# Sums of decayed traces in a two-layer conditioning and mixture kernel: additions on GpSimd against accumulating transfers within the chip

## The chip, the cores and the metric

One core of a Trainium2 chip runs the kernel. The metric is the device time of one execution in microseconds, the median of several runs. Lower is better.

## The reference, cut to what matters

The kernel computes a language-adapted feed-forward mixture over 8 batches of 512 tokens and 256 channels, then a temporal conditioning with a second mixture of 64 experts. The change touches the conditioning alone, and there this part:

```python
def causal_ema(b, tau_raw):
    alpha = jnp.exp(-jax.nn.softplus(tau_raw)).astype(b.dtype)
    def step(h, bt):
        h = alpha * h + bt
        return (h, h)
...
gated = x * wg
mod = 0.5 + jax.nn.sigmoid(jnp.einsum('bth,dh->btd', h1, Wn2) + bn2)
traces = jax.vmap(lambda tau, m: causal_ema(gated * m[..., None], tau))(tau_raws, jnp.moveaxis(mod, -1, 0))
blend_w = jax.nn.softmax(blend, axis=0)
temporal = jnp.einsum('dbtc,dc->btc', traces, blend_w)
gate = jax.nn.sigmoid(jnp.einsum('btc,ec->bte', temporal, Wtemp) + btemp)
soma = jax.nn.gelu(jnp.einsum('btc,ec->bte', x, Wsoma) + bsoma, approximate=False)
out = jnp.einsum('btc,ec->bte', soma * gate, Wout)
```

Eight time constants (D = 8) give eight traces for each batch; `temporal` is their weighted sum. The sum of traces, seven additions for each batch, is what the change moves.

## The kernel before, in words

The kernel has three stages: layer 0 (to about 538 us of the span), the conditioning of layer 1 (to about 830 us), and the 64 experts of layer 1. Five engines run programs of their own, and semaphores order them.

In the conditioning a batch is a tile of 128 partitions (channels) x 2 halves x 512 tokens in float32, 4 KB for each partition, 512 KB in all. The blend weight is folded into the input, so the traces have only to be added. For each batch `b` and each time constant `d` from 0 to 7 the work runs through three engines:

- ScalarE, `weighted` (L879), scales the gated input with the blend weight into `gb`, of which there are two buffers.
- GpSimd, `drive_of` (L628), multiplies it with the modulation `md` into one of three `drive` buffers. It waits for the scan of three drives earlier.
- VectorE, `scan_unit` (L1239), scans each half along time, two instructions for each drive. Trace 0 goes straight to `acc[b % 2]`; traces 1 to 7 go to one of three `trace` buffers, which must have been added before they are written again.
- `add_trace` adds trace `d` to `acc[b % 2]`. GpSimd does it for `d` = 1, 2, 3, 5, 6 and 7 (L636), VectorE for `d` = 4 (L1248); in the last batch VectorE also does 6 and 7. Each addition waits for its scan and for the addition before it, through the semaphore `c_add`.

When addition 7 is through, TensorE's `temp_in` projects `acc` with `wtemp` (L1629), ScalarE applies the tanh (`gate_out`, L920), and VectorE's `gate_soma` (L1270) multiplies it with `soma`. The statistics of the normalisation follow (`stats`, L1277 and L1280), then four small GpSimd instructions in `rstd_of` (L614 to L619).

The order on each engine is written out by hand, as a list in its `step(b)`, and three batches overlap in a step. GpSimd's step `b` is: `rstd_of(b - 2)`, drive 7 and addition 5 of batch `b - 1`, drives 0 and 1 of batch `b`, additions 6 and 7 of `b - 1`, drive 2, addition 1, drives 3 and 4, additions 2 and 3, drives 5 and 6 of `b`. VectorE's step has scans 0 and 1, `shared_b`, the context scan, `pick` (its cast is L1303), scan 2, `gate_soma`, scan 3, `shared_a`, `route_weights` (L1331), scan 4, `stats`, addition 4, scan 5, `gate_in` (L1263), scan 6, `finish` (L1338) and scan 7.

The sync engine's queue issues the loads and stores: the modulation, broadcast to all partitions (L435, 1 MB, twice a step), the batch's rows (L420, L446), and the stores (L451, L455). In its step 3 it also issues the first five experts' weights (L427, L428). GpSimd issues indirect transfers in the other stages (L587, L602, L713, L720) and one direct transfer with addition, of 4 MB, at the very end (L737).

Of the kernel before, what the change touches and what calls it, by code (L numbers as in the profile page):

```python
# [31 lines left out]
D = 8  # L32
# [14 lines left out]
def level(m, per=1):  # L47
    return (m + 1 + CREDIT) * per
# [15 lines left out]
def build(nc, t):  # L64
# [20 lines left out]
    with ctx:  # L85
# [241 lines left out]
        c_mst = sem("c_mst", 16)  # L327
        c_mdl = [sem(f"c_mdl{n}", 16) for n in range(2)]
        c_pad, e_pad = sem("c_pad", 0), sem("e_pad", 0)
        c_in = [sem(f"c_in{p}", 16) for p in range(2)]  # L330
# [38 lines left out]

        def added(b, d):  # L370

            return level((D - 1) * b + d - 1)

# [8 lines left out]
        def _(sp):  # L382
# [74 lines left out]
            def c_step(b):  # L457
# [18 lines left out]
                if b == B:  # L476
                    z_store(B - 2)

                    sp.wait_ge(c_add, added(B - 1, D - 1))
                    for e in range(OWN + HEADS, FREED):  # L480
                        e_load(e)
# [24 lines left out]
        def _(pool):  # L506
# [124 lines left out]
            def add_trace(b, d):  # L631
                pool.wait_ge(c_scan, level(D * b + d))
                if d > 1:
                    pool.wait_ge(c_add, added(b, d - 1))
                pool.drain()
                G.tensor_tensor(acc[b % 2][:, :, :], acc[b % 2][:, :, :], trace[((D - 1) * b + d - 1) % TRACES], ALU.add).then_inc(c_add, 1)  # L636
# [14 lines left out]
            def step(b):  # L651
# [6 lines left out]
                if ahead(b):  # L658
                    drive_of(b, 0)
                if ahead(b):  # L660
                    drive_of(b, 1)
                if on(b - 1) and b != B:
                    add_trace(b - 1, 6)
                if on(b - 1) and b != B:
# [9 lines left out]
                if on(b):  # L674
                    add_trace(b, 2)
                if on(b):
                    add_trace(b, 3)
                if on(b):
                    drive_of(b, 5)
                if on(b):  # L680
                    drive_of(b, 6)
                if b == B:

                    pool.wait_ge(c_add, added(B - 1, D - 1))
                    for r in range(FREED):
# [364 lines left out]
        def _(dve):  # L1050
# [177 lines left out]
            def scan_unit(b, d):  # L1228
# [5 lines left out]
                else:  # L1234
                    n = (D - 1) * b + d - 1
                    dve.wait_ge(c_add, level(n - TRACES))
                    dst = trace[n % TRACES]
# [5 lines left out]
            def add_trace(b, d):  # L1243
                dve.wait_ge(c_scan, level(D * b + d))
                if d > 1:
                    dve.wait_ge(c_add, added(b, d - 1))
                dve.drain()
# [253 lines left out]
        def _(pe):  # L1501
# [152 lines left out]
            def temp_in(q):  # L1654
                pe.wait_ge(c_add, added(q, D - 1))
                if q + 2 < B:
# [278 lines left out]
```

## Time and profile before

| | |
|---|---|
| median of 3 runs | 1130.76 us (1129.94 to 1133.33) |
| the profiled execution, its time | 1128.04 us |
| the profiled execution, its span | 1126.3 us |
| VectorE busy over the span | 743.0 us (66%) |
| GpSimd busy over the span | 663.5 us (59%) |
| TensorE busy over the span | 939.8 us (83%) |

The table's shares are averages over three stages with different limits. For this change only the conditioning counts, so it is to be read by its steps. In the rows, PE is TensorE, PEld its weight loads, DVE VectorE, ACT ScalarE, POOL GpSimd and SP the sync engine; "wide" is the buffer in which `drive`, `trace`, `acc`, `gb` and others lie. What stands in brackets behind a row of the timeline is the idle time ahead of it and what ended it.

### The profile page before, as it was taken

The numbers are of one execution on the slowest core, as the hardware profiler recorded it, in microseconds if no ns is written. First come the engines' busy times: TensorE is split into PE (matmuls) and PEld (weight loads), VectorE is DVE, ScalarE is ACT, GpSimd is POOL, SyncE is SP. The second block draws the span as 40 slices with busy tenths as digits, with TensorE's granted clock in tenths as the row PEclk, the third lists the DMA queues.
The fourth block names the chain that finished last, engine by engine and source line by source line (L and its number), as shares of the span: only waits on it lengthen the run. The fifth ranks groups of instructions, "written<-read, shape, count | busy, mean of one in ns | idle before, by whom it ended". The sixth has DMA issues, their size and how long they took to land. (4 is left out here: it accounts for less than half of the span.)

```text
span 1126.3 us, 15057 instructions
## 1 busy us (share of the span) xinstructions
PE 939.8 (83%) x4616; PEld 676.5 (60%) x4616; DVE 743.0 (66%) x1523; ACT 470.3 (42%) x843; POOL 663.5 (59%) x495
## 2 busy tenths in 40 slices
PE   5981399999999999988478899998777798999960
PEld 3761289998999899973134555554454465556540
DVE  3547366766676667534578999999874786777620
ACT  2331055445544555354346665666422132233320
POOL 1113415545554555325899999999850577777870
PEclk9885599999999999998689999999876999999995
DMA  2559514444443443223212652344348599997558
GB/s 78 149 185 368 157 47 90 94 117 86 89 96 77 120 90 52 29 57 108 86 51 75 214 159 87 111 136 119 104 140 317 172 254 254 270 260 152 94 72 157
DMA packets 90455, 151.28 MB, mean 134 GB/s; under 512 B 15816, under 2 KB 72848, under 8 KB 87248
## 3 DMA queue, kind: packets, MB, share of 16 engines
q1 hardware_dynamic: 55184, 95.46, 25.9%
q0 software_dynamic: 25104, 39.86, 20.5%
q10 hardware_dynamic: 10096, 15.10, 4.1%
q8 instruction: 33, 0.54, 0.2%
q14 instruction: 38, 0.31, 0.1%
HBM read 115.37 MB, written 43.42 MB: 141 GB/s over the span
## 5 line engine op out<-in xcount | busy, mean ns | idle before, releaser
L628 POOL TENSOR_TENSOR wide<-wide 128x1024 f32<-128x1024 f32 x64 | 156.5, 2459 | 32.1 <-issue 32.1
L1239 DVE TENSOR_TENSOR_SCAN wide<-bank,wide 128x512 f32<-128x512 f32 x128 | 149.4, 1209 | 21.8 <-POOL wide L628 21.8
L855 ACT ACTIVATE h_raw<-bank,b 128x512 f32<-128x512 f32 x128 | 87.9, 688 | 168.3 <-PE bank L1602 165.9
L1194 DVE TENSOR_TENSOR h_lo<-h_raw,h_hi 128x512 fp32r<-128x512 f32 x128 | 87.2, 692 | 93.9 <-ACT h_hi L859 93.9
L1617 PE MATMUL bank<-w_hi,h_hi 128*128 128x256 f32 x512 | 144.3, 282 | 0.1
L1617 PE MATMUL bank<-w_lo,h_hi 128*128 128x256 f32 x512 | 142.1, 277 | 0.0
L1617 PE MATMUL bank<-w_hi,h_lo 128*128 128x256 f32 x512 | 142.0, 277 | 0.0
L602 POOL DMA_INDIRECT x_rows<-ob,put x64 | 110.9, 1733 | 27.3 <-issue 14.3
L636 POOL TENSOR_TENSOR wide<-wide 128x1024 f32<-128x1024 f32 x46 | 108.5, 2358 | 11.9 <-issue 8.2
L879 ACT ACTIVATE wide<-wide,blend 128x512 f32<-128x512 f32 x128 | 84.1, 716 | 59.9 <-POOL wide L628 56.5
L1602 PE MATMUL bank<-ex_hi,w_hi 128*128 128x512 f32 x256 | 100.3, 392 | 4.9 <-issue 4.9
L1602 PE MATMUL bank<-ex_hi,w_lo 128*128 128x512 f32 x256 | 101.3, 396 | 0.0
L1602 PE MATMUL bank<-ex_lo,w_hi 128*128 128x512 f32 x256 | 101.0, 394 | 0.0
L1617 PEld LDWEIGHTS bank<-w_hi,h_hi 128*128 128x128 f32 x512 | 96.8, 189 | 1.6 <-issue 1.1
L1617 PEld LDWEIGHTS bank<-w_lo,h_hi 128*128 128x128 f32 x512 | 96.9, 189 | 0.3 <-issue 0.2
L1617 PEld LDWEIGHTS bank<-w_hi,h_lo 128*128 128x128 f32 x512 | 96.7, 189 | 0.0
L713 POOL DMA_INDIRECT xg<-z_rows,slots x64 | 63.5, 992 | 54.1 <-DVE slots L1377 36.1
L596 POOL COPY put<-idxT 128x4 int32<-128x4 int32 (+1 forms) x16 | 3.0, 185 | 137.8 <-DVE ob L1183 137.8
L587 POOL DMA_INDIRECT xg<-n_rows,take x64 | 67.4, 1052 | 28.2 <-issue 14.9
L859 ACT ACTIVATE h_hi<-h_raw 128x512 fp32r<-128x512 f32 x128 | 77.9, 621 | 0.0
L1038 ACT ACTIVATE ys<-bank 128x256 f32<-128x256 f32 x64 | 24.5, 383 | 98.0 <-DMA out<-ys,slots 43.3
L720 POOL DMA_INDIRECT odd_rows<-ys,slots x32 | 51.4, 1606 | 17.3 <-ACT ys L1038 8.2
(230 smaller groups left out, 2034.1 us busy)
## 6 DMA issues: line engine op xcount, KB each, us to landing
wide<-in_mwp SPq DMA_DIRECT2D x40, 512.0 KB, 4.4
wide<-m_rows SPq DMA_DIRECT2D x16, 1024.0 KB, 4.8
w1s<-in_fW SPq DMA_DIRECT2D x8, 1024.0 KB, 5.0
w2s<-in_fW SPq DMA_DIRECT2D x8, 1024.0 KB, 5.3
own<-in_mwp SPq DMA_DIRECT2D x15, 512.0 KB, 4.2
z_rows<-zrow SPq DMA_DIRECT2D x8, 640.0 KB, 7.1
head<-in_mwp SPq DMA_DIRECT2D x9, 512.0 KB, 4.4
xt<-in_x SPq DMA_DIRECT2D x8, 512.0 KB, 3.9
```

What stands on the lines that cost most here:

```text
L587: G.indirect_dma_start(xg0[p][:, j, :], None, n0_rows[:, :], bass.IndirectOffsetOnAxis(ap=take[p][:, j:j + 1], axis=0)).then_inc(b_got[p], 16)
L602: G.indirect_dma_start(x1_rows[:, :], bass.IndirectOffsetOnAxis(ap=put[p][:, j:j + 1], axis=0), ob[p][:, j, :], None, compute_op=ALU.add). ...
L628: G.tensor_tensor(drive[n % DRIVES], gb[d % 2], md[d // HD][:, d % HD, :].unsqueeze(1).to_broadcast([P, CT, S]), ALU.mult).then_inc(c_u, 1)
L636: G.tensor_tensor(acc[b % 2][:, :, :], acc[b % 2][:, :, :], trace[((D - 1) * b + d - 1) % TRACES], ALU.add).then_inc(c_add, 1)
L713: G.indirect_dma_start(xg1[i][:, :], None, z_rows[:, :], bass.IndirectOffsetOnAxis(ap=slots[:, e:e + 1], axis=0)).then_inc(e_got[i], 16)
L855: A.activation(h1_raw[f % 4][:, :], bank[:, 2 + f % 4, :], ACT.Gelu_apprx_tanh, bias=b1_0[:, bass.ds(e, 1), f]).then_inc(b_h, 1)
L859: A.activation(h1_hi[:, f - 1, :], h1_raw[(f - 1) % 4][:, :], ACT.Copy).then_inc(b_hi, 1)
L879: o = A.activation(gb[d % 2][:, c, :], gated2[b % 2][:, c, :], ACT.Copy, scale=blend[:, c, d:d + 1])
L1194: V.tensor_tensor(h1_lo[:, f, :], h1_raw[f % 4][:, :], h1_hi[:, f, :].bitcast(F32), ALU.subtract).then_inc(b_lo, 1)
L1239: o = V.tensor_tensor_scan(dst[:, c, :], decay[:, d:d + 1].to_broadcast([P, S]), drive[(D * b + d) % DRIVES][:, c, :], 0.0, ALU.mult, ALU.add)
L1602: o = T.matmul(bank[:, 2 + f % 4, :], w[q][:, at], x[p][:, c, :], start=(c == 0 and n == 0), stop=(c == CT - 1 and n == 2))
L1617: o = T.matmul(rows4(6)[:, j, :], x[:, f, rows], w[q][:, f * H:(f + 1) * H], start=(f == 0 and n == 0), stop=(f == FT0 - 1 and n == 2))
```

## The change

For all batches but the last, additions 1, 2, 3, 5, 6 and 7 are made by a transfer that GpSimd issues: it reads the trace in the chip's memory and adds it to `acc`. Each transfer adds 16 to the semaphore `c_acc` of its buffer when it has landed, and whoever waited for `c_add` waits for that. Addition 4 stays on VectorE, and the last batch is added as before. On GpSimd, addition 6 moves ahead of drive 1, and drive 5 moves ahead of addition 3.

```diff
@@ -326,6 +326,7 @@
         c_no = sem("c_no", TT)
         c_mst = sem("c_mst", 16)
         c_mdl = [sem(f"c_mdl{n}", 16) for n in range(2)]
+        c_acc = [sem(f"c_acc{p}", 0) for p in range(2)]
         c_pad, e_pad = sem("c_pad", 0), sem("e_pad", 0)
         c_in = [sem(f"c_in{p}", 16) for p in range(2)]
         c_xr, c_zst, c_ost = sem("c_xr", 16), sem("c_zst", 16), sem("c_ost", 16)
@@ -367,9 +368,17 @@
 
             return 0 < n < B
 
-        def added(b, d):
-
-            return level((D - 1) * b + d - 1)
+        BY_DMA = (1, 2, 3, 5, 6, 7)
+
+        def wait_added(eng, b, d):
+
+
+            if b == B - 1:
+                eng.wait_ge(c_add, level(B - 1 + d - 1))
+            elif b >= 0 and d in BY_DMA:
+                eng.wait_ge(c_acc[b % 2], 16 * (len(BY_DMA) * (b // 2) + BY_DMA.index(d) + 1))
+            elif b >= 0:
+                eng.wait_ge(c_add, level(b))
 
         def conditioning(first, step):
 
@@ -476,7 +485,7 @@
                 if b == B:
                     z_store(B - 2)
 
-                    sp.wait_ge(c_add, added(B - 1, D - 1))
+                    wait_added(sp, B - 1, D - 1)
                     for e in range(OWN + HEADS, FREED):
                         e_load(e)
                 if ahead(b + 1):
@@ -631,7 +640,11 @@
             def add_trace(b, d):
                 pool.wait_ge(c_scan, level(D * b + d))
                 if d > 1:
-                    pool.wait_ge(c_add, added(b, d - 1))
+                    wait_added(pool, b, d - 1)
+                if b < B - 1:
+                    pool.dma_start(acc[b % 2].rearrange("p c s -> p (c s)"), trace[((D - 1) * b + d - 1) % TRACES].rearrange("p c s -> p (c s)"),
+                                   accum_op=ALU.add).then_inc(c_acc[b % 2], 16)
+                    return
                 pool.drain()
                 G.tensor_tensor(acc[b % 2][:, :, :], acc[b % 2][:, :, :], trace[((D - 1) * b + d - 1) % TRACES], ALU.add).then_inc(c_add, 1)
 
@@ -657,10 +670,10 @@
                     add_trace(b - 1, 5)
                 if ahead(b):
                     drive_of(b, 0)
+                if on(b - 1) and b != B:
+                    add_trace(b - 1, 6)
                 if ahead(b):
                     drive_of(b, 1)
-                if on(b - 1) and b != B:
-                    add_trace(b - 1, 6)
                 if on(b - 1) and b != B:
                     add_trace(b - 1, 7)
                 if ahead(b):
@@ -674,14 +687,14 @@
                 if on(b):
                     add_trace(b, 2)
                 if on(b):
+                    drive_of(b, 5)
+                if on(b):
                     add_trace(b, 3)
-                if on(b):
-                    drive_of(b, 5)
                 if on(b):
                     drive_of(b, 6)
                 if b == B:
 
-                    pool.wait_ge(c_add, added(B - 1, D - 1))
+                    wait_added(pool, B - 1, D - 1)
                     for r in range(FREED):
                         G.memset(wdb[r][0:P - FR, :], 0.0)
                     pool.wait_ge(c_om, level(B - 1))
@@ -1233,7 +1246,7 @@
                     dst = acc[b % 2]
                 else:
                     n = (D - 1) * b + d - 1
-                    dve.wait_ge(c_add, level(n - TRACES))
+                    wait_added(dve, (n - TRACES) // (D - 1), (n - TRACES) % (D - 1) + 1)
                     dst = trace[n % TRACES]
                 for c in range(CT):
                     o = V.tensor_tensor_scan(dst[:, c, :], decay[:, d:d + 1].to_broadcast([P, S]),
@@ -1243,7 +1256,7 @@
             def add_trace(b, d):
                 dve.wait_ge(c_scan, level(D * b + d))
                 if d > 1:
-                    dve.wait_ge(c_add, added(b, d - 1))
+                    wait_added(dve, b, d - 1)
                 dve.drain()
                 V.tensor_tensor(acc[b % 2][:, :, :], acc[b % 2][:, :, :], trace[((D - 1) * b + d - 1) % TRACES], ALU.add).then_inc(c_add, 1)
 
@@ -1652,7 +1665,7 @@
                 o.then_inc(c_h1m, 1)
 
             def temp_in(q):
-                pe.wait_ge(c_add, added(q, D - 1))
+                wait_added(pe, q, D - 1)
                 if q + 2 < B:
                     pe.wait_ge(c_x1T, level(q + 2))
                 pe.wait_ge(c_fin, level(q - 2))
```

## Rows read from the trace of the kernel before

**Rows 1.** Busy time by batch step: stretch, length, engines (instructions), TensorE clock, DMA share, GB/s.

```profile
...
593.91:631.02 37.11, 34.43 (x114) 19.42 (x114) 32.84 (x51) 22.55 (x36) 35.73 (x19) 0.95 0.31 104
631.02:668.14 37.12, 33.25 (x116) 18.30 (x114) 36.09 (x54) 23.84 (x37) 35.74 (x19) 1.00 0.64 197
668.14:705.60 37.46, 34.91 (x116) 19.15 (x114) 35.85 (x54) 23.84 (x37) 35.79 (x19) 0.95 0.36 117
```

**Rows 2.** The page's costliest groups, GpSimd's drives (L628) and additions (L636).

```profile
...
L628 POOL TENSOR_TENSOR wide<-wide 128x1024 f32<-128x1024 f32 x64 | 156.5, 2459 | 32.1 <-issue 32.1
...
L636 POOL TENSOR_TENSOR wide<-wide 128x1024 f32<-128x1024 f32 x46 | 108.5, 2358 | 11.9 <-issue 8.2
```

**Rows 3.** GpSimd's timeline in one step: start, length, instruction, idle before it.

```profile
...
670.65 2.37 POOL L636 TENSOR_TENSOR wide<-wide 128x1024 f32<-128x1024 f32 x1 [0.16 <-issue]
672.98 4.65 POOL L628 TENSOR_TENSOR wide<-wide 128x1024 f32<-128x1024 f32 x2
677.79 2.36 POOL L636 TENSOR_TENSOR wide<-wide 128x1024 f32<-128x1024 f32 x1 [0.16 <-issue]
680.66 2.35 POOL L636 TENSOR_TENSOR wide<-wide 128x1024 f32<-128x1024 f32 x1 [0.52 <-POOL wide L636]
...
702.73 1.20 POOL L614 TENSOR_SCALAR veps<-mv_b 128x4 f32<-128x4 f32 x1
...
705.60 2.35 POOL L628 TENSOR_TENSOR wide<-wide 128x1024 f32<-128x1024 f32 x1
```

**Rows 4.** VectorE's timeline in the same step.

```profile
...
668.55 1.19 DVE L1263 SCALAR_TENSOR_TENSOR wide<-bank,head 128x1024 f32<-128x1024 f32 x1
...
673.03 6.97 DVE L1239 TENSOR_TENSOR_SCAN wide<-bank,wide 128x512 f32<-128x512 f32 x6
...
690.42 1.22 DVE L1270 SCALAR_TENSOR_TENSOR wide<-bank,wide 128x1024 f32<-128x1024 f32 x1
...
701.87 0.38 DVE L1280 BATCH_NORM_AGGREGATE mv_b<-stat 128x2 f32<-128x6 f32 x4
702.50 1.34 DVE L1248 TENSOR_TENSOR wide<-wide 128x1024 f32<-128x1024 f32 x1 [0.26 <-issue]
703.76 2.32 DVE L1239 TENSOR_TENSOR_SCAN wide<-bank,wide 128x512 f32<-128x512 f32 x2
```

**Rows 5.** ScalarE's timeline: the tanh behind the gate projection.

```profile
...
687.24 1.24 ACT L920 ACTIVATE bank<-bank,btemp_h 128x512 f32<-128x512 f32 x2 [2.95 <-PE bank L1629]
```

**Rows 6.** Three lines' instructions: shortest, median and longest duration in ns.

```profile
...
L614 POOL TENSOR_SCALAR veps<-mv_b x8: 233/1202/1212, 591.9 to 844.1; 128x4 f32<-128x4 f32 x8
...
L1303 DVE CAST mask_all<-mask x8: 723/1362/1881, 612.3 to 856.1; 128x256 bf16<-128x256 f32 x8
...
L1331 DVE TENSOR_TENSOR zrow<-mask,wsum x8: 425/1754/1761, 621.9 to 861.4; 128x256 f32<-128x256 f32 x8
```

**Rows 7.** Issues by GpSimd, ns, and us from an issue's start to its landing: L587, L737.

```profile
...
L587 POOL DMA_INDIRECT xg<-n_rows,take x64: 942/985/1701, 121.3 to 450.2; - x64
...
DMA to landing us min/median/max: 2.7/2.8/3.9
...
L737 POOL DMA_DIRECT2D out<-odd_rows x1: 1155/1155/1155, 1101.8 to 1101.8; - x1
...
DMA to landing us min/median/max: 23.1/23.1/23.1
```

**Rows 8.** Short stretches; the last two figures are DMA share and GB/s.

```profile
...
671.00:674.00 3.00, 3.00 (x3) 0.50 0.67 273
674.00:677.00 3.00, 3.00 (x4) 0.95 1.00 362
677.00:680.00 3.00, 3.00 (x3) 1.00 0.74 245
...
683.00:692.00 9.00, 8.76 (x21) 1.00 0.00 0
...
1110.00:1118.00 8.00, 0.00 (x0) 0.00 (x0) 0.00 (x0) 0.00 (x0) 0.00 (x0) 0.50 1.02 213
```

## The prediction

> **What bounds the kernel now.** I first cut the conditioning stage, the only one that changes, into its batch steps, each from one start of drive 7 on GpSimd to the next [rows 1]. The steps take 37.11, 37.12 and 37.46 us, 37.2 on average. In the last of them GpSimd is busy for 35.79 us and VectorE for 35.85, so both engines are full. TensorE's busy time, 34.91, is close behind. The grouped view [rows 2] says of what GpSimd's time consists: 64 drives of 2.46 us and 46 additions of 2.36, of which a middle step has eight and six. GpSimd's timeline [rows 3] has no gap over 0.6 us that waits for another engine. It sets the pace, and VectorE [rows 4] has almost nothing to spare: taking work from GpSimd alone can bring at most what VectorE leaves.
>
> **The sum, part by part.**
>
> *Removed:* 42 of the 46 additions on GpSimd (36 in the six middle steps, three in step 0, three in step 7), 2.36 us each [rows 2], 14.2 us a step. With them goes the drain ahead of each, 0.16 us of idle time [rows 3].
>
> *Added on GpSimd:* 42 issues of a direct transfer with addition. The one such issue here takes 1.16 us, an indirect gather 0.94 to 1.70 [rows 7]. At 1.16, six are 7 us a step, so GpSimd's own work falls from 35.8 to about 28.6 us. Were that all, VectorE alone would bound.
>
> *Added waits:* each transfer but a batch's first waits until the one ahead has landed, and GpSimd stands still meanwhile, with the later drives queued behind it. So what counts is T, from the start of an issue to the landing of 512 KB. No row shows a transfer of this kind within the chip. Lower end: a gather of 128 KB into the chip lands 2.7 us after its issue starts; the remaining 384 KB at the 213 GB/s of the closing 4 MB addition [rows 7, 8] take 1.85, together 4.55. Upper end: that closing addition lands after 23.1 us; less 3584 KB at 213 GB/s (17.2), 5.9 stay. The destination speaks for the lower end, the addition for the upper one: I take the middle, 5.2.
>
> *Collisions:* from 671 to 680 us, just behind gate_in at 668.55 [rows 4], the sync engine's loads and stores keep the DMA engines busy, 0.67, 1.00 and 0.74 [rows 8]. Addition 5 would run there from about 670 to 677 and addition 6 to 683; addition 7 falls into a stretch of share 0.00. Sharing the engines fully would add the transfer's own data time (512 KB at 213 GB/s, 2.5 us) to each of the two; I take half, 1.2. Then 5, 6 and 7 take 6.4 + 6.4 + 5.2 = 18.0 us. The step with the first weight loads has a DMA share of 0.64 rather than 0.36 [rows 1]: one more collision, 1.2 us once.
>
> *The loop that closes:* additions 5, 6 and 7 of a batch stand between its drive 7 and its gate projection. From VectorE's end of statistics (702.25 [rows 4]): GpSimd's four small instructions, 2.87 (702.73 to 705.60 [rows 3]), drive 7, 2.35, the three transfers, then projection and tanh. Today addition 7 ends at 683.01 [rows 3] and the tanh at 688.48 [rows 5]: 5.47. Then VectorE from the gate product at 690.42 to the end of statistics at 702.25: 11.83. Today these pieces have 1.94 us of slack (688.48 to 690.42). Sum: 2.87 + 2.35 + 5.47 + 11.83 + 0.1 for semaphores = 22.6, plus 18.0 = 40.6 us a step.
>
> *Relief:* two of these pieces are longer today than need be. The route weights' product takes 1.75 us in the median and 0.43 at the least, and GpSimd's first small instruction 1.20 against 0.23 [rows 6]; the short forms come where the other of the two engines is idle. Up to 2.3 us come back; since GpSimd still computes for half of a step, I take 1.1. The step then lasts **39.5 us**, 2.3 over today.
>
> *Moved:* addition 6 now stands ahead of drive 1, so drive 1 waits for addition 5 to land. It ends at 2.87 + 2.35 + 6.4 + 1.16 + 2.35 = 15.1 us after the statistics. VectorE wants it for the third of the six scan pairs from 673.03 on [rows 4], at 677.67, 12.9 after the statistics (702.25 less 37.46): 2.2 us late. That is a second loop, of VectorE's order: 37.5 - 0.6 idle + 2.2 - 1.1 = 38 us, below the first. Moving drive 5 ahead of addition 3 costs nothing: it fills time in which GpSimd would wait for addition 2. The third loop, add 4 and scan 5 on VectorE (1.34 + 2.32 [rows 4]), two transfers at 6.4, issue and drive 2 (3.5), addition 1 with two drives beside it (5.9), two more (5.2 and 6.4), is 37.5. Nothing else is longer; the trace buffers' waits come in the same order.
>
> *Total:* six middle steps x 2.3 = 14, plus 1.2 = 15 us. I cost steps 0 and 7 at nothing: each has three transfers in place of six, and step 7 keeps three additions on GpSimd; if that cover is gone they are one middle step together, 2.3. The profiled execution took 1128.04 us, so it would become 1143; the median shown, 1130.76, lies 2.7 above it, which gives **1146 us**.
>
> **Rules weighed.** GpSimd's small instruction takes 1.20 us beside a busy VectorE and 0.23 beside an idle one [rows 6], so one engine does hold the other up. The Trainium skill (SBUF — State Buffer, "SBUF: two separate sides") says that GpSimd cannot write the descriptors of its own transfers while certain VectorE instructions hold the port pair that both use. By the rule each issue may come late, which would make the sum that of the blocked case below instead of 1146. The trace bears it out in part: gather issues range from 0.94 to 1.70 us [rows 7].
>
> **Rivals.**
>
> *Faster, VectorE becomes the bound.* Mechanism: the transfers meet nobody and land fast, T = 4.55. Then the first loop is 22.6 + 13.7 - 2.3 = 34.0, and VectorE's own work decides: 35.85, less half of what its cast (1.36 in the median to 0.72) and the product (1.75 to 0.43) can shed [rows 6], 1.0, plus 0.6 of waits, is 35.4. Six steps x 1.8 is 11 saved: 1120 us. It decides below a mean T of 5.25 (37.2 - 22.6 + 1.1 = 15.7 for three). For it speaks the SBUF destination. Against it: the DMA share of 1.00 where additions 5 and 6 fall, and the closing addition, which moves 213 GB/s while the share is full, whereas plain transfers reach 362 in a full slice [rows 8]. The Trainium skill (DMA: Bandwidth & Descriptors, "Anatomy of one DMA — SWDGE (gpsimd) path") gives 2.0 us plus bytes over 436 GB/s for a transfer from GpSimd; an estimate by it is 3.2 us for 512 KB, and the kernel would come out at this rival's 1120. The trace agrees for the gather and contradicts it for the addition: by the rule 4 MB would take 11.6 us, and it takes 23.1.
>
> *No change.* The collisions cost nothing while T is 5.2: 22.6 + 15.6 - 1.1 = 37.1 us a step, 1130.
>
> *Blocked issues, clearly slower.* Each of the three issues in the loop grows by 0.76 us (0.94 to 1.70 [rows 7]): 2.3 more a step, 41.8, 28 us in all plus 1.2: 1160. It decides if the issues fall on VectorE's cast and products; most of VectorE's time is scans, so I hold it less likely.
>
> **How the numbers follow.** A change of 0.3%, 3.4 us, is about what measuring this kernel can tell from none. Forecast 0.45 (1134 to 1156, from T between 5.0 and 6.2 with the collisions); blocked issues or full collisions 0.18; no change 0.10; VectorE-bound 0.27. Slower 0.63, same 0.10, faster 0.27. The two ends give 1120 and, with T = 5.9 and half collisions, 6 x 4.4 + 1.2 over 1131, 1159; blocked issues on top reach 1172. The range is 1118 to 1168.
>
> **What would show it.** In the profile after: no addition of GpSimd but four; GpSimd busy near 75% of a step, and its idle time put down to the transfer; landings of 5 to 6.5 us, longer for additions 5 and 6; TensorE's first projection with wtemp waiting for that transfer; the gate product on VectorE waiting for the tanh; steps of 39 to 40 us. A landing below 5 us throughout, with VectorE without gaps, would prove the forecast wrong; so would issues near 2 us, the other way.

## The result, and the profile after

The changed kernel takes 1222.6 us (1219.6 to 1223.5, four runs) against 1130.4 before: a ratio of 1.078, with an interval of 1.075 to 1.082. The sign of the forecast was right and its size was not: 15 us were forecast, and 92 came. The profiled execution has a span of 1217.9 us against 1126.3.

First the page of the changed kernel: groups of the conditioning (line, engine, instruction; busy time and mean ns; idle time ahead and its releaser) and the issue row of the new transfers.

```profile
DMA wide<-wide 18%; DMA odd_rows<-ys,slots 4%; POOL wide L637 2%; POOL xg L726 2%; POOL out L733 1%; POOL odd_rows L733 1%; SPq L436 1%; DMA z_rows<-zrow 1%; DMA out<-ys,slots 1%; DMA xg<-z_rows,slots 1%; SPq L437 1%; DVE wide L1252 1%; DVE xgT L1482 1%; PE bank L1858 0%; DVE wide L1276 0%
...
L637 POOL TENSOR_TENSOR wide<-wide 128x1024 f32<-128x1024 f32 x64 | 166.5, 2623 | 75.0 <-issue 75.0
...
L645 POOL DMA_DIRECT2D wide<-wide x42 | 40.1, 956 | 83.5 <-DMA wide<-wide 74.0
...
wide<-wide POOLq DMA_DIRECT2D x42, 512.0 KB, 5.1
```

Read the last row alone and the change looks harmless: 5.1 us in the median from issue to landing, almost the 5.2 of the prediction. But the chain that ended last runs for 18% of the span, some 220 us, through these transfers. Before, no transfer of the conditioning stood in it. And GpSimd's drives, L637, have 75.0 us of idle time ahead of them against 32.1 in [rows 2].

Now GpSimd's timeline over one step, the counterpart of [rows 3], from drive 7 to the small instructions.

```profile
705.66 2.35 POOL L637 TENSOR_TENSOR wide<-wide 128x1024 f32<-128x1024 f32 x1
707.95 0.93 POOL L645 DMA_DIRECT2D wide<-wide  x1
709.34 2.36 POOL L637 TENSOR_TENSOR wide<-wide 128x1024 f32<-128x1024 f32 x1 [0.46 <-issue]
718.22 0.90 POOL L645 DMA_DIRECT2D wide<-wide  x1 [6.52 <-DMA wide<-wide]
...
724.46 0.89 POOL L645 DMA_DIRECT2D wide<-wide  x1 [2.96 <-DMA wide<-wide]
...
727.35 1.22 POOL L645 DMA_DIRECT2D wide<-wide  x1
727.94 3.02 POOL L637 TENSOR_TENSOR wide<-wide 128x1024 f32<-128x1024 f32 x1
737.00 2.35 POOL L637 TENSOR_TENSOR wide<-wide 128x1024 f32<-128x1024 f32 x1 [6.04 <-issue]
739.30 0.87 POOL L645 DMA_DIRECT2D wide<-wide  x1
...
744.38 0.88 POOL L645 DMA_DIRECT2D wide<-wide  x1 [1.82 <-DMA wide<-wide]
744.97 2.67 POOL L637 TENSOR_TENSOR wide<-wide 128x1024 f32<-128x1024 f32 x1
748.24 0.23 POOL L623 TENSOR_SCALAR veps<-mv_b 128x4 f32<-128x4 f32 x1 [0.60 <-DVEq L1294]
748.44 0.22 POOL L624 TENSOR_SCALAR shift_b<-mv_b 128x4 f32<-128x4 f32 x1
754.48 1.90 POOL L626 TENSOR_TENSOR rstd_b<-veps,mhalf 128x4 f32<-128x4 f32 x1 [5.81 <-issue]
```

The step runs from 705.66 to 756.91 (the next drive 7): 51.25 us against 37.2 in [rows 1] and 39.5 forecast. Counted at the small instruction L626, the six intervals between steps are 50.1, 56.4, 51.0, 51.7, 50.4 and 50.7 us, together 310; at L617 of the kernel before they are together 225. These 85 us are nearly the whole of the 92. (This sum over six intervals is what the experiments are measured with below.)

The forecast had the waits for additions 5 and 6. Three things it did not have are in this timeline: addition 5 lands only 9.7 us after its issue, where 6.4 was forecast; GpSimd stands for 6.04 us ahead of drive 4 and no transfer is named; and between two of the small instructions, L624 and L626, where there is nothing but a drain, it stands for 5.81 us. The chain of waits of the same step, from which pieces are left out here, puts them in a row (start, length, what).

```profile
707.95 9.72 DMA wide<-wide
...
718.22 5.71 DMA wide<-wide
...
724.46 4.10 DMA wide<-wide
728.57 2.39 POOL wide L637
730.95 6.03 issue
737.00 0.50 POOL wide L637
737.50 1.80 issue
739.30 4.54 DMA wide<-wide
743.89 0.48 issue
744.38 9.71 DMA wide<-wide
```

Five of the six transfers are here, all but addition 1, one behind the other: 5, 6, 7, 2, 3. Each that waits for the one ahead is issued 0.5 us after that one's landing (717.68 to 718.22). What stands between 7 and 2 is told by ScalarE, whose row [rows 5] showed before, and by TensorE ahead of it.

```profile
729.09 5.25 PE L1642 MATMUL bank<-wide,wtemp 128*128 128x512 f32 x8 [7.91 <-DMA wide<-wide]
```

```profile
734.38 1.24 ACT L933 ACTIVATE bank<-bank,btemp_h 128x512 f32<-128x512 f32 x2 [10.88 <-PE bank L1642]
735.54 2.55 ACT L892 ACTIVATE wide<-wide,blend 128x512 f32<-128x512 f32 x4
```

The projection starts when addition 7 has landed (729.09), the tanh follows it at 734.38, and the weighting for drive 4 stands behind the tanh in ScalarE's written-out order. So drive 4 of one batch waits for addition 7 of the batch before it. The whole step of 51.25 us then adds up, from drive 7 to drive 7: the five transfers 34.3, three starts behind a landing 1.6, the projection until the tanh's start 5.3, tanh and weighting until drive 4 starts 2.6, drives 7 and 4 4.6, and from the landing of addition 3 to the next drive 7 2.8.

The projection itself is longer too. Its eight matmuls take 5.25 us here, after 7.91 us in which TensorE stood idle, and took 3.70 before:

```profile
683.50 3.70 PE L1629 MATMUL bank<-wide,wtemp 128*128 128x512 f32 x8
```

The clock granted to TensorE is 0.50 from 729 to 732 us, the lower of its two levels, and 1.00 from 683 to 686 us of the kernel before. So the wait for addition 7 costs 1.1 us more than its own length: from its end to the tanh's start it is 5.3 us, and was 4.2 [rows 3, 5].

The wait of drive 4 behind the tanh is theory Q, from ScalarE's queue. Against it stood theory D (GpSimd's drain behind an issued transfer costs) and theory C (the collisions with the sync engine's transfers cost).

### The profile page after: what moved, and what is told of

Read it like the earlier page. It is cut to its first block, busy times and chain, and to the rows that moved or that the text cites. A ratio compares the mean times of both kernels' runs of the same rounds, so it can differ in the third digit from the quotient of the medians.

```text
span 1217.9 us, 15012 instructions
## 1 busy us (share of the span) xinstructions
PE 948.0 (78%) x4616; PEld 681.1 (56%) x4616; DVE 742.9 (61%) x1523; ACT 470.2 (39%) x843; POOL 599.0 (49%) x495
## 4 chain that ended last, share of the span: by engine, by line
DMA 25%; issue 12%; POOL 7%; DVE 4%; SPq 2%; PE 2%; POOLq 1%; DVEq 1%; ACT 1%; ACTq 0%
DMA wide<-wide 18%; DMA odd_rows<-ys,slots 4%; POOL wide L637 2%; POOL xg L726 2%; POOL out L733 1%; POOL odd_rows L733 1%; SPq L436 1%; DMA z_rows<-zrow 1%; DMA out<-ys,slots 1%; DMA xg<-z_rows,slots 1%; SPq L437 1%; DVE wide L1252 1%; DVE xgT L1482 1%; PE bank L1858 0%; DVE wide L1276 0%
## 5 line engine op out<-in xcount | busy, mean ns | idle before, releaser
L637 POOL TENSOR_TENSOR wide<-wide 128x1024 f32<-128x1024 f32 x64 | 166.5, 2623 | 75.0 <-issue 75.0
L1642 PE MATMUL bank<-wide,wtemp 128*128 128x512 f32 x64 | 40.8, 796 | 56.2 <-DMA wide<-wide 56.2
L645 POOL DMA_DIRECT2D wide<-wide x42 | 40.1, 956 | 83.5 <-DMA wide<-wide 74.0
## 6 DMA issues: line engine op xcount, KB each, us to landing
z_rows<-zrow SPq DMA_DIRECT2D x8, 640.0 KB, 10.3
```

The lines of the kernel that those rows point to most:

```text
L637: G.tensor_tensor(drive[n % DRIVES], gb[d % 2], md[d // HD][:, d % HD, :].unsqueeze(1).to_broadcast([P, CT, S]), ALU.mult).then_inc(c_u, 1)
L1642: o = T.matmul(bank[:, o_banks + n, :], w[:, c, n * P:(n + 1) * P], src[c], start=(c == 0), stop=(c == k - 1))
```

## The experiments

Beside these runs the kernel before took 1131 to 1134 us in the median; ratios are to that, and differences in us to the changed kernel's 1222.6.

### The tanh behind the weighting, and the drains away

`act_order` moves one call on ScalarE:

```diff
-                if on(b - 1):
-                    gate_out(b - 1)
                 if on(b):
                     weighted(b, 4)
                 if on(b):
                     weighted(b, 5)
+                if on(b - 1):
+                    gate_out(b - 1)
```

> The changed kernel, with one thing moved: on ScalarE the gate's tanh of the batch before stands behind the weighting for drives 4 and 5 instead of ahead of the weighting for drive 4. Theory Q (ScalarE's written-out order ties two loops into one: drive 4 waits for its weighting, which is queued behind the tanh, which waits for the landing of addition 7 and the projection, so that five transfers, 5, 6, 7, 2 and 3, stand in one loop): GpSimd's idle time of 6 us ahead of drive 4 goes, the step falls from 51 us to about 45 (the loop is then additions 5 and 6, drive 2, addition 1, 2 and 3), 1185 us. Theory D (GpSimd's drain behind an issued transfer is what costs) and theory C (collisions with the sync engine's transfers alone): drive 4 is off the path, no change within 5 us of 1222.

Measured: 1198.0 us (two runs), 25 less than the changed kernel; the intervals are 46.8 to 48.2 us but for one of 51.9, together 289. Drives 3 and 4 follow each other without a gap:

```profile
720.16 5.30 POOL L637 TENSOR_TENSOR wide<-wide 128x1024 f32<-128x1024 f32 x2
728.42 0.88 POOL L645 DMA_DIRECT2D wide<-wide  x1 [2.95 <-DVE wide L1252]
```

The link is real. Less came back than expected (3.7 us a step rather than 6), since addition 2 now waits for a scan of VectorE instead, which is late itself. Ahead of that scan stands VectorE's cast, and beside the two drives it lasts 4.37 us (721.70 to 726.07), against 1.44 in the changed kernel's step above.

`no_drain` replaces the two drains among the small instructions:

```diff
-                G.tensor_scalar(veps1[:, :], mv1[:, :, 1], 4 * EPS, None, ALU.add)
-                G.tensor_scalar(shift1[:, :], mv1[:, :, 0], -1.0, None, ALU.mult)
-                pool.drain()
-                G.tensor_tensor(rstd1[:, :], veps1[:, :], mhalf[:, :], ALU.pow)
-                pool.drain()
+                G.tensor_scalar(veps1[:, :], mv1[:, :, 1], 4 * EPS, None, ALU.add).then_inc(c_rr, 1)
+                G.tensor_scalar(shift1[:, :], mv1[:, :, 0], -1.0, None, ALU.mult).then_inc(c_rr, 1)
+                pool.wait_ge(c_rr, 3 * q + 2)
+                G.tensor_tensor(rstd1[:, :], veps1[:, :], mhalf[:, :], ALU.pow).then_inc(c_rr, 1)
+                pool.wait_ge(c_rr, 3 * q + 3)
```

> The changed kernel, with the two drains in the small instructions of rstd_of replaced by waits for a semaphore that those instructions raise. Theory D: the drain waits until the transfer issued last has landed, 5.8 us a step, and this is on the path: 6 x 5.8 less, about 1188 us. Theory Q: the idle time of 5.8 us between the small instructions goes (if the drain waits for the transfer at all), but addition 4 and scan 5 wait for the same landing on VectorE and end at the same time as drive 7 did, so the total falls by 0 to 2 us a step: 1212 to 1222 us.

Measured: 1201.0 us (1198.4 and 1203.7), between the two theories: 22 us less, where theory D gave about 35 and theory Q at most 11. The idle time is gone (the second small instruction starts at 694.72, the third at 695.02). But addition 5 then waits for VectorE's scan 5, which is itself behind addition 4 and so behind the same landing. Its row reads:

```profile
704.30 0.93 POOL L646 DMA_DIRECT2D wide<-wide  x1 [5.66 <-DVE wide L1253]
```

That is what theory Q expected. The gain that it did not expect may come from drive 7, which is now early (696.30), so that what waits for it starts earlier; that is not shown. In this step addition 5 landed after 4.6 us and addition 6 took the 9.9 us in its place. What makes the 22 us was not separated.

`act_no_drain` is both edits together.

> The changed kernel with both edits of the runs before it: ScalarE's tanh behind the weighting for drives 4 and 5, and rstd_of without drains. If queue order (51 to 47.5 us a step) and drain (to 48.5) are separate links of one loop, their gains add: about 44 to 45 us a step, 1180 us. If both gains came from the same slack, it stays at 47, 1195 us.

Measured: 1190.0 us (1186.1 and 1193.9), intervals of 46 to 54 us, together 292, no less than with either edit alone (289 and 291). The 8 us under `act_order` stand ahead of the first interval (the first L627 starts at 589.2 instead of 597.6 us). So the gains overlap. In both kernels VectorE waits some 6 us a step for drive 1, which is queued behind the landing of addition 5, and has at most 3.6 us of idle time from there to the statistics: once the tanh is out of the way, this second loop of the prediction is nearly as long as the first.

### The collisions

`small_loads` cuts the modulation's loads, from the changed kernel; the later batches compute with stale modulation:

```diff
+                w = HD * S if b == 0 else 16
-                sp.dma_start(md[n].rearrange("p d s -> p (d s)"), ...
+                sp.dma_start(md[n].rearrange("p d s -> p (d s)")[:, 0:w], ...
```

> The changed kernel, with the modulation's two broadcast loads of each batch after the first cut from 1 MB to the first 16 columns (8 KB); the computation then uses stale modulation, which is the part left out. Theory C (collisions): additions 3 and 5, which now land after 9.7 us, land in 5 to 7 us, 3 to 4 us less each; the step falls from 51 to about 44 to 46 us, 1185 to 1195 us. Theory Q takes the same gain for both, since both stand in its loop. If the other transfers (stores, rows) cause the long landings, addition 5 stays above 8 us and only addition 3 gains.

Measured: 1184.8 us, 38 less, intervals together 278. The landing of addition 3 comes 6.6 us after its issue instead of 9.7 (727.54 to the drain's end at 734.54, less the 0.4 us that the drain's end lies behind a landing), and addition 5 lands in less than 5.6. That load was the larger part of both collisions. The one of addition 6 grew in its place: it lands after 6.8 and 9.1 us in two steps that I read. In the changed kernel the sync engine's issues stand right beside them:

```profile
708.09 0.32 SPq L444 DMA_DIRECT2D wide<-m_rows  x1
...
744.35 0.33 SPq L444 DMA_DIRECT2D wide<-m_rows  x1
744.78 0.38 SPq L460 DMA_DIRECT2D z_rows<-zrow  x1
```

Addition 5 was issued at 707.95 and addition 3 at 744.38: each within 0.2 us of a load of 1 MB. For addition 5 this is built in: the load into the second half of the modulation waits for drive 7, which reads that half last, and addition 5 is what GpSimd does right behind drive 7. The other side pays too. The store of 640 KB (L460) takes 10.3 us to land in the median, against 7.1 before, and the modulation's load 6.4 against 4.8.

`act_no_drain_small_loads` has the three edits together.

> All three edits together: tanh behind two weightings, no drains in rstd_of, modulation loads of later batches cut to 8 KB (stale modulation is the part left out). If queue order, drain and collisions are the whole difference to the prediction's step, the step comes down to 39 to 40 us, which is what the prediction had, about 1145 us. If it stays above 43, something is still missing.

Measured: 1174.4 us, intervals together 278, three of the six 45. Something was still missing, and the timeline named it: addition 6, at 688.87, was followed by addition 7 only at 698.62, beside the row loads and the output store, which the sync engine issued between 686.27 and 687.32. So `act_no_drain_all_small` cuts these as well; most of the output is then not written, which is left out.

> The kernel of act_no_drain_small_loads, with the sync engine's row loads and output store of the stage cut as well, to 64 columns of a quarter of the rows (their later rows are stale and most of the output isn't written, which is left out). There addition 6 still landed after 9.7 us, beside just these transfers, and the step was 45 us. If collisions explain that landing, additions 5 to 7 land after 4.6 to 5 us, the first loop of the prediction gives 22.6 + 3 x 5 = 37.6, and the step is 38 to 40 us, 1140 us. If 9.7 us has another cause, such as transfers of one queue behind each other, the step stays at 45.

Measured: 1152.4 us, three intervals of 40.6 to 41.3 and three of 42.2, 45.4 and 49.8, together 260. GpSimd's timeline, and below it VectorE's:

```profile
713.59 2.35 POOL L645 TENSOR_TENSOR wide<-wide 128x1024 f32<-128x1024 f32 x1
715.89 0.93 POOL L653 DMA_DIRECT2D wide<-wide  x1
...
721.49 0.88 POOL L653 DMA_DIRECT2D wide<-wide  x1 [2.10 <-DVE wide L1260]
...
727.53 0.88 POOL L653 DMA_DIRECT2D wide<-wide  x1 [2.77 <-DVE wide L1260]
...
744.30 0.88 POOL L653 DMA_DIRECT2D wide<-wide  x1 [1.79 <-DMA wide<-wide]
...
752.00 0.23 POOL L631 TENSOR_SCALAR veps<-mv_b 128x4 f32<-128x4 f32 x1 [4.43 <-DVEq L1302]
```

```profile
724.79 2.34 DVE L1260 TENSOR_TENSOR_SCAN wide<-bank,wide 128x512 f32<-128x512 f32 x2 [1.45 <-POOL wide L645]
...
733.37 3.53 DVE L1324 CAST mask_all<-mask 128x256 bf16<-128x256 f32 x1
...
744.81 3.05 DVE L1352 TENSOR_TENSOR zrow<-mask,wsum 128x256 f32<-128x256 f32 x1
```

The collisions are gone: the six transfers of this stretch land after 4.5 to 5.5 us. Additions 6, 7 and 3 still wait for the transfer ahead of them. The rows of 6 and 7 name a scan, but the transfers 5 and 6 landed at 721.0 and 727.0, 0.5 us ahead of the issues, and the scans 6 and 7 had ended before. Two loops of the prediction close here at the same time. The first goes through additions 5, 6 and 7: from the end of the statistics (710.78) 5.1 us to addition 5, then 5.6 and 6.0 to additions 6 and 7, 4.6 until 7 has landed (732.1), 6.7 until the tanh has ended (738.82), and 13.1 from the gate product (738.89) until the next statistics are through (752.00), 41.2 in all. The prediction's terms for the same, with T = 5, give 37.6. Of the 3.6 us between them, the two starts behind a landing are 1.1, projection and tanh 1.2 (the eight matmuls take 5.40 us), and VectorE's part behind the gate product 1.3, with a product of 3.05 us in it. The second is VectorE's own order: it starts scan 1 at 724.79, when drive 1 has ended, and works to the statistics without a wait, so without the tanh it would have been no sooner. The prediction has 38 for this one. Its cast and product take 6.6 us here, and had 1.4 and 1.8 in the median before [rows 6]. So even with everything but the transfers themselves taken off, the change costs 4 us a step, in the starts behind landings, in TensorE's slower projection and in VectorE held up beside GpSimd's drives.

### The additions free of charge

`free_adds` raises the semaphore in place of the transfer; 42 additions are not computed:

```diff
-                    pool.dma_start(acc[b % 2]..., accum_op=ALU.add).then_inc(c_acc[b % 2], 16)
+                    pool.sem_inc(c_acc[b % 2], 16)
```

> The changed kernel, with the 42 transfers left out and their semaphore raised at once: 42 of the 56 trace additions are not computed. It gives what the change could bring at best. By the sum of the prediction VectorE then bounds, 35.4 us a step and 1120 us; by theory Q too, since nothing of the loop is left. If the step stayed above 45 us, the issue order of the change and not its transfers would be to blame.

Measured: 1106.6 us, 2.4% under the kernel before (ratio 0.976, 0.967 to 0.985). The step is 35.5 to 36.0 us, but for the first of 37.3: the 35.4 that the prediction gave as VectorE's floor was right for a step. The time as a whole is 13 us lower than that floor's 1120: the steps in which the pipeline fills gain as much (the first L626 starts at 579.6 us, L617 before at 592.6). The order of the instructions is thus not to blame, and everything between 1107 and 1223 us comes with the transfers: their issues, their waits and what they do to the neighbours.

### One half of the additions, and the moved drives

`only_5_6_7` computes additions 1, 2 and 3 on GpSimd again, with the waits adapted (`BY_DMA = (5, 6, 7)`).

> The changed kernel with additions 5, 6 and 7 alone as transfers; 1, 2 and 3 are computed on GpSimd again. The chain that ScalarE's order closes is then three transfers long, not five: 2 and 3 drop out (4.5 + 9.7 + 1 us against 2.6 + 2.4 of arithmetic, 10 us less), and there is no transfer in flight at the drain. Theory Q: 51 less 10, about 41 to 42 us a step, 1160 us.

Measured: 1202.8 us (1198.3 and 1207.4), intervals of 45 to 53 us, together 289. I had expected 41 to 42: wrong. In the step that I read, GpSimd still stands for 3.40 us ahead of drive 4 (732.62), so the link through the tanh is there. From drive 4 to the next drive 7 it takes 15.0 us instead of 19.9: 5 us come back and not 10, because drives 5 and 6, which ran beside transfers 2 and 3, now stand in the same row as additions 2 and 3. Additions 5 and 6 landed after 9.1 and 6.4 us, and the drain ahead of addition 1 stood for 1.57 us until addition 7 had landed. Three transfers in GpSimd's own queue cost 70 us of the 92 that six cost.

`old_order` undoes the two moves in the changed kernel.

> The changed kernel with drive 1 back ahead of addition 6 and drive 5 back behind addition 3. Drive 1 then fills part of the wait for addition 5 (collided, 9.7 us), drive 5 no longer fills the wait for addition 2. By theory Q the chain of the five transfers stands still in both: two drives beside addition 5 and none beside 6; one drive, 2.35 us, moves out from under addition 2 but behind addition 3's issue, where it delays nothing. Within 1 us a step of 51, 1216 to 1230 us.

Measured: 1227.4 us, 0.4% slower than the changed kernel, intervals together 314. As expected: the moves are not what costs. They bring about 5 us at most; the kernel before differed by 2.6 us between the two sets of runs (1130.4 and 1132.9).

### A single transfer, and what a drain waits for

The rest asks whether one transfer that is well covered would pay. All of these start from the kernel before, with `BY_DMA` cut to one or two additions and the other waits as they were.

`one_transfer` makes addition 1 alone a transfer.

> The kernel before, with addition 1 of each batch but the last as a transfer, nothing else: two drives of 2.35 us stand between its issue and the next addition, and a transfer lands after 4.6 us. GpSimd's step falls from 35.8 to 34.5 us of work, VectorE's floor is 35.5 us as in the run without additions. Theory Q (only waits in a chain cost, one covered transfer costs its issue): 35.6 to 36.2 us a step, 1118 to 1124 us, faster than the kernel before. Theory that transfers harm in themselves (port or drain): no faster than before, 1130 or more.

Measured over ten runs: 1134.8 us, a ratio of 1.003 (0.9997 to 1.006): no gain, against theory Q. The transfer lands after 4.6 us in the later steps, beside its drives, as planned. The steps take 37.5 to 38.9 us in the profiled execution. VectorE has no idle time in the step that I read and is longer by its cast, which takes 2.63 us beside the issue and drive 3 (in [rows 6] the median was 1.36).

`one_transfer_drain` adds a drain:

```diff
                                    accum_op=ALU.add).then_inc(c_acc[b % 2], 16)
+                    pool.drain()
                     return
```

> The kernel with one transfer, and a drain directly behind its issue. If the drain waits until the transfer has landed, GpSimd's gap between the issue and drive 3 is about 4 us (4.6 from the issue's start), against under 0.2 without it, and the step grows by what the two drives had covered, to about 38 to 39 us, 1140 to 1145 us. If the drain waits for GpSimd's own arithmetic alone, the gap stays under 0.5 us and the time is that of the kernel with one transfer.

```profile
697.99 0.92 POOL L648 DMA_DIRECT2D wide<-wide  x1
702.85 4.66 POOL L640 TENSOR_TENSOR wide<-wide 128x1024 f32<-128x1024 f32 x2 [3.93 <-ACT wide L896]
```

```profile
DMA to landing us min/median/max: 4.6/4.6/6.9
```

Measured: 1144.1 us, four of the six steps 39.1 to 39.5 us. The issue starts at 697.99, the transfer lands 4.6 us later, at 702.6, and drive 3 starts at 702.85. (The row names ScalarE as the releaser, but in `one_transfer` the same drive started 0.68 us after the issue's start.) GpSimd's drain waits for its own transfer in flight. And with GpSimd standing still, VectorE's cast takes 0.73 us in the median.

`only_3` and `only_3_7` put the transfer where nobody on GpSimd waits for it.

> The kernel before, with addition 3 alone as a transfer. Nobody on GpSimd waits for it: two drives follow, VectorE takes addition 4 some 7 us later, and the cast on VectorE, which lasted 2.6 us beside the issue of addition 1, is over by then. If VectorE's own work bounds and depends on what GpSimd does beside it, the step is 36 to 37 us, 1120 to 1127 us. If a covered transfer brings nothing whatever its place, 37.5 us and 1131 or more.

> The kernel before, with additions 3 and 7 as transfers. Addition 7 is waited for by the projection alone, which has 1.9 us to spare, and lands 2.3 us later than the arithmetic would end; the drain ahead of addition 1 comes 4.8 us behind its issue. GpSimd has 2.9 us less work a step. Expected 35.8 to 36.8 us a step, 1116 to 1126 us; no better than addition 3 alone if VectorE bounds there already.

Measured: 1146.3 us (ratio 1.013, 1.009 to 1.016) and 1172.3 us (1.034, 1.030 to 1.037). Both expectations fell, on the wrong side. In `only_3`, whose steps take mostly 40.6 to 40.9 us, VectorE and GpSimd read:

```profile
705.28 5.37 DVE L1347 TENSOR_TENSOR zrow<-mask,wsum 128x256 f32<-128x256 f32 x1
```

```profile
704.72 0.93 POOL L648 DMA_DIRECT2D wide<-wide  x1 [0.55 <-POOL wide L652]
705.40 4.95 POOL L640 TENSOR_TENSOR wide<-wide 128x1024 f32<-128x1024 f32 x2
714.78 0.23 POOL L626 TENSOR_SCALAR veps<-mv_b 128x4 f32<-128x4 f32 x1 [4.43 <-DVEq L1297]
```

In `only_3_7`, whose steps take 42 us, the product lasts up to 5.26 us, and the drain ahead of addition 1 stands for 1.47 us until transfer 7 has landed.

The product, which needs 0.43 us alone, lasts 5.37. It ends 0.3 us after drives 5 and 6, which run in one piece from 705.40 to 710.35. The transfer itself landed at 709.6, so two theories stayed: P, that VectorE waits for a gap in GpSimd's run of instructions, and T, that the transfer holds it off. `only_3_gap` gives GpSimd a pause behind each drive:

```diff
                                 md[d // HD][:, d % HD, :]..., ALU.mult).then_inc(c_u, 1)
+                pool.wait_ge(c_u, level(n))
```

> The kernel with addition 3 alone as a transfer, in which GpSimd, after each drive, waits for that drive's own semaphore before it goes on, a pause of about 0.2 us. Theory P (VectorE's instructions with two inputs in the chip's memory wait until GpSimd's unbroken run of instructions ends): the product gets in between drives 5 and 6, 2.6 to 3.0 us instead of 5.4, the step falls from 40.8 to about 38.5 us, 1133 us. Theory T (the transfer in flight holds VectorE off): the product stays at about 5 us, until the landing.

```profile
706.08 3.07 DVE L1348 TENSOR_TENSOR zrow<-mask,wsum 128x256 f32<-128x256 f32 x1
```

```profile
706.22 5.15 POOL L640 TENSOR_TENSOR wide<-wide 128x1024 f32<-128x1024 f32 x2
```

Measured: 1136.6 us, 38.5 us a step, the product 3.07 us, as P said and against T: it ended at 709.15, 2.2 us before the second drive did and 1.5 us before the transfer landed (710.6). A pause of 0.2 us between two drives gave VectorE back 2.3 us. The Trainium skill (SBUF — State Buffer, "SBUF: two separate sides") says that the loser of the port pair waits for the winner's whole instruction. In `only_3` it waited for two; in the kernel before, shown next, for one.

But P is not the whole of it. There GpSimd goes from addition 3 to drive 5 without a pause, and VectorE's product gets in:

```profile
695.60 2.35 POOL L636 TENSOR_TENSOR wide<-wide 128x1024 f32<-128x1024 f32 x1 [0.23 <-POOL wide L636]
697.91 4.84 POOL L628 TENSOR_TENSOR wide<-wide 128x1024 f32<-128x1024 f32 x2
```

```profile
696.48 1.76 DVE L1331 TENSOR_TENSOR zrow<-mask,wsum 128x256 f32<-128x256 f32 x1
```

It ends at 698.24, 0.3 us after the addition. In `one_transfer` it gets in between drives 5 and 6, which follow each other without a pause as well, behind a computed addition 3: the drives run from 742.90 to 747.93 in one piece, the product from 744.36 to 745.72.

So in these two VectorE waits for one instruction, pause or none. In the steps that I read it waited for two only where GpSimd had issued a transfer just ahead of them (`only_3`, `only_3_7`, and the cast in `act_order` and `act_no_drain_all_small`), and then a pause between the two let it in. Why the issue matters stays open.

`before_gap` is the control: the kernel before with the same pauses, and no transfer.

> The kernel before, unchanged but for the same pause behind each drive. No transfer is in it. Theory P: the product and the cast lose less, but GpSimd bounds here and pays 0.2 us for each pause that is new (behind drives 0, 3, 5 and 6): 37.6 to 38.2 us a step, 1133 to 1138 us, and the product shorter than 1.75 us or as long. Theory T says nothing of it.

Measured: 1136.1 us (1.002, 0.9995 to 1.005), 37.5 us a step, the product 1.75 us as before. Where no transfer is issued, the pause brings VectorE nothing.

Last, `only_2` makes addition 2 alone a transfer, with drive 5 ahead of addition 3, so that GpSimd stands still for a moment just where VectorE needs it; `only_2_gap` adds the pauses.

> The kernel before with addition 2 alone as a transfer and drive 5 ahead of addition 3, so that the drain ahead of addition 3 holds GpSimd for the 1.3 us until the landing, and VectorE finds GpSimd idle there. GpSimd's work and wait together are 35.5 us. Theory P: the cast meets drives 3 and 4 as before, the product meets addition 3 or drive 6 alone: 36 to 37 us a step, 1122 to 1130 us. If it is 1131 or more, no place of a single transfer among those tried pays.

> The kernel with addition 2 alone as a transfer, with the pause of about 0.2 us behind each drive. Theory P: the cast, 2.2 us beside drives 3 and 4, gets in between them as in only_3_gap; it was 1.8 there. VectorE gains up to 0.5 us, GpSimd pays up to 0.8 us out of the 1.9 us that it waited for the statistics in some steps. 36.8 to 37.3 us a step, 1127 to 1132 us, no clear difference to only_2. A ratio whose interval lies wholly under 1 would show that one transfer can pay.

Measured: 1130.0 us (0.997, 0.993 to 1.0002) and 1131.3 us (0.998, 0.995 to 1.0005), with mostly 37.0 us a step and the product at 0.43 us in the median in `only_2`. Both intervals just include 1. If one transfer pays at all, it is less than can be told here. The kernel before stands.

## Why the prediction was wrong

- **What bounds before** was right: `free_adds` shows VectorE's floor at 35.5 us a step where 35.4 was worked out, and the kernel before, with GpSimd full, stands above it at 37.2.
- **The landing of a transfer that meets nobody** was right within its bounds. It takes 4.5 to 4.6 us, the lower end (4.55), not the 5.2 of the middle. The prediction's other estimate, 3.2 us, is 1.3 short of that; for the gather the same formula gives 2.3, where [rows 7] have 2.8, so the trace bore it out less than was said. GpSimd's issue takes 0.88 us in the median, not 1.16. What the sum put at 0.1 in all is the 0.5 us from a landing to the issue that waits for it, three times in the chain of a step.
- **The collisions** were mis-sized, in the term "I take half, 1.2": a transfer that meets the 1 MB load lands after 9.7 us, 5.2 more, which is above even the full sharing of 2.5 us that the prediction had as its upper end. The other side's 1.6 to 2.5 MB, issued within 5 us, are served at the same time, which fits the size but was not separated. And the meeting moves in a slower step: addition 3, which the sum had only in its third loop, met the modulation's load and the store in each of the steps that I read. `small_loads` gives 38 us for the modulation's load alone.
- **The loops** were judged one by one, and the step that failed is the sentence "Nothing else is longer". ScalarE's queue, in which the tanh stands ahead of the weighting for drive 4, ties the first and the third loop into one with five transfers. The prediction had read one row of ScalarE and not its order. `act_order` gives 25 us for it.
- **The drain** was taken as 0.16 us of idle time. Behind a transfer in flight it lasts until the landing, 5.8 us in the small instructions. `no_drain` gives 22 us, which overlaps with the 25 of `act_order`: both together give 33.
- **The first loop itself**, with the other causes taken off, takes 41.2 us instead of 37.6: the starts behind a landing, and two terms carried over from before that grew by 1.2 and 1.3. In the changed kernel the first of them, projection and tanh, takes 6.5 us (729.09 to 735.62) where 5.47 stood, at a granted TensorE clock of 0.50 behind the wait. The second loop, put at 38 us, is as long as the first there. The forecast's slower sign did not hang on the other errors.
- **Relief**: the product did fall to 0.43 us in the median of the changed kernel, as worked out. But the multiplication two instructions ahead of it (L1338, 0.51 us before) rose to 2.46, so nothing came back on the whole.
- **Blocked issues**: this rival is refuted as a cause. The issues were shorter in the median, not longer, and the longest of the 42 took 1.56 us; it is VectorE that was held off.
- **The chances' interval** doesn't follow from its own terms: with T = 5.0 and 6.2 and the collisions the sum gives 1142 and 1164 us, not 1134 and 1156. And the six scan instructions from 673.03 are three pairs, not six; the start of the third, 677.67, is read rightly.

The forecast's range ended at 1168 us because the bounds of the terms were added up, but not the loops; it even ended short of the 1172 to which the prediction's own worst terms add up. What the causes come to: counted by the six intervals, of the 310 us of the changed kernel, 50 go with queue order, drains and collisions (`act_no_drain_all_small`, 260), and a further 44 with the transfers alone and what they do to VectorE (`free_adds`, 216). The kernel before has 225.

## What to carry to other kernels

A chain of dependent transfers costs its latency times its length, so a transfer is to be put only where its result isn't needed until after its landing, and never behind another one. Before a wait is added on one engine, read the written-out queue of every engine that consumes what that engine makes: here a tanh ahead of an unrelated scaling tied two batches together and made a chain of three into one of five. And where the issue of a transfer takes the place of arithmetic, read the neighbour's instructions too: VectorE's cast and product, which had got in between two of GpSimd's instructions, then waited for two of them. Last, look at an engine that waits for the slow thing and computes behind it: TensorE came back from its wait at half its clock.

## What the runs showed of the hardware that was not expected

- GpSimd's drain waits for its own transfers: 3.9 us of idle time directly behind an issue with a landing at 4.6 us, 5.8 us in the changed kernel and 1.6 in `only_5_6_7`, against 0.16 us where nothing is in flight.
- VectorE's instruction with two inputs in the chip's memory (the product, 0.43 us alone) lasted 5.4 us beside two drives of GpSimd that followed a transfer's issue and each other without a pause, and 3.1 us when 0.2 us lay between them. Without an issue ahead it took 1.4 and 1.8 us, pause or none.
- TensorE's eight matmuls of the projection took 5.25 us at a granted clock of 0.50 behind 7.91 us of idle time, and 3.70 us at 1.00.
- A 512 KB addition within the chip lands after 4.6 us alone and after 9.7 us beside a load of 1 MB and further transfers of the sync engine. Its median of 5.1 us hides this, since in most steps only two or three in six meet them, and those stand in the chain.
